# A Flamingo block on one core: the first stage in four pipeline steps, with both layer norms applied by ScalarE

## What is computed

```
x = x + tanh(g_xattn[0]) * L0_xattn(layernorm(x), ctx)      # stage A
x = x + tanh(g_ffn[0])   * L0_ffn(layernorm(x))             # stage B, 8 experts, top 2
x = x + tanh(g_xattn[1]) * L1_xattn(layernorm(x), ctx, ctx) # stage C, 16 heads, mask
x = x + tanh(g_ffn[1])   * L1_ffn(layernorm(x))             # stage D, 8 experts, top 2, and a shared one

layernorm(x) = (x - mean) / sqrt(var + 1e-5)
L0_xattn: q = x1 w_q', k = x2 w_k', v = x2 w_v'; softmax(q k' / sqrt(128)) v
L0_ffn:   logits = x Wg; softmax; the two best experts per token, weights summing to one
```

## Time and profile before

| | |
|---|---|
| median of 3 runs | 770.51 us (768.73 to 771.58) |
| the profiled execution | 768.41 us, of which the span of its instructions is 766.6 us |
| mean granted clock of PE in it | 0.91 of 2.4 GHz |
| stage A in the profiled execution | from 0 to 138.8 us, where stage B's first PE instruction starts |
| busy in the span | PE 656.9 us, DVE 574.7, ACT 427.4, POOL 92.7 |

### The profile page before, as it was taken

How to read it: one execution, slowest core, us unless ns; L and a number is a source line. 1 busy time by engine, 2 the same in 40 slices (tenths; PEclk the granted TensorE clock), 3 DMA queues, 4 the chain that set the end, 5 groups by cost and what they waited for, 6 DMA issues and landing times.

```text
span 766.6 us, 12867 instructions
## 1 busy us (share of the span) xinstructions
PE 656.9 (86%) x4158; PEld 508.3 (66%) x4158; DVE 574.7 (75%) x1211; ACT 427.4 (56%) x657; POOL 92.7 (12%) x121
## 2 busy tenths in 40 slices
PE   5665764799999999995799989989988379999996
PEld 4544553587787778773576766766766258888884
DVE  3777566788898889887586866866866678888885
ACT  3233321577777777773376666665766045555553
POOL 3344221200000000002001011011011100000000
PEclk9677565799999999998599999999999579999998
DMA  5313100000000000002333413413400000000000
GB/s 159 101 53 106 31 8 0 1 1 0 1 0 0 0 0 0 0 1 80 81 99 101 109 37 94 111 37 89 110 1 1 0 1 2 14 14 14 27 15 28
DMA packets 23698, 29.24 MB, mean 38 GB/s; under 512 B 3313, under 2 KB 17522, under 8 KB 23666
## 3 DMA queue, kind: packets, MB, share of 16 engines
q1 hardware_dynamic: 23666, 28.84, 13.3%
HBM read 19.99 MB, written 8.85 MB: 38 GB/s over the span
## 4 chain that ended last, share of the span: by engine, by line
PE 66%; DVE 18%; issue 5%; POOL 5%; ACT 4%; DVEq 1%; DMA 0%; SPq 0%; ACTq 0%; POOLq 0%
PE psum L371 12%; PE psum L373 12%; PE psum L372 12%; PE psum L1156 5%; DVE xn L300 3%; PE psum L1171 3%; DVE stats L281 2%; POOL rstd L293 2%; PE psum L1146 2%; PE psum L360 2%; PE psum L1147 2%; PE psum L1448 2%; PE psum L858 2%; PE psum L349 1%; DVE xl L332 1%
## 5 line engine op out<-in xcount | busy, mean ns | idle before, releaser
L1262 ACT ACTIVATE c_pt<-psum 77x512 f32<-77x512 f32 x128 | 74.9, 586 | 60.5 <-PE psum L1156 60.0
L371 PE MATMUL psum<-xh,w_hi 128*128 (+1 forms) x248 | 102.1, 412 | 2.1 <-DVE d_hr L1536 2.1
L372 PE MATMUL psum<-xl,w_hi 128*128 (+1 forms) x248 | 99.4, 401 | 0.0
L373 PE MATMUL psum<-xh,w_lo 128*128 (+1 forms) x248 | 99.1, 400 | 0.0
L813 DVE TENSOR_TENSOR b_hl<-b_hs,b_hh 128x1024 fp32r<-128x1024 f32 x64 | 78.2, 1222 | 17.9 <-ACT b_hh L807 17.9
L916 ACT ACTIVATE b_hr<-psum,b1s 128x512 f32<-128x512 f32 x128 | 81.1, 686 | 17.1 <-PE psum L373 17.1
L958 DVE TENSOR_TENSOR b_hs<-b_hr,psum 128x1024 f32<-128x1024 f32 x64 | 78.2, 1222 | 12.1 <-ACT b_hr L916 10.9
L807 ACT ACTIVATE b_hh<-b_hs 128x1024 fp32r<-128x1024 f32 x64 | 68.0, 1062 | 34.1 <-PE psum L373 34.1
L1156 PE MATMUL psum<-ident,c_pf 128*77 128x128 f32 x512 | 75.0, 283 | 0.0
L1156 PEld LDWEIGHTS psum<-ident,c_pf 128*77 128x77 f32 x512 | 58.3, 149 | 15.0 <-issue 10.2
L1322 DVE TENSOR_REDUCE c_mx<-psum 128x8 f32<-128x616 f32 x64 | 51.1, 799 | 17.0 <-PE psum L1147 16.0
(11 more groups left out here) (205 smaller groups left out, 1287.5 us busy)
## 6 DMA issues: line engine op xcount, KB each, us to landing
w_hi<-c_q_spread SPq DMA_DIRECT2D x24, 256.0 KB
stage<-in_weights SPq DMA_DIRECT2D x8, 576.0 KB, 4.2
c_q_spread<-w_hi SPq DMA_DIRECT2D x8, 512.0 KB, 3.4
ctxg<-in_ctxT SPq DMA_DIRECT2D x16, 156.0 KB, 4.2
c_k_spread<-w_lo SPq DMA_DIRECT2D x8, 312.0 KB, 2.2
x_all<-in_x SPq DMA_DIRECT2D x8, 256.0 KB, 3.0
out_dram<-x_all SPq DMA_DIRECT2D x8, 256.0 KB, 2.3
c_kb<-c_k_spread SPq DMA_DIRECT2D x48, 39.0 KB
```

The lines of the kernel that those rows point to most:

```text
L371: pe.matmul(o, wh, h, start=start, stop=False)
L372: pe.matmul(o, wh, l, start=False, stop=False)
L373: return pe.matmul(o, wl, h, start=False, stop=stop)
L1262: a_.activation(pt[:, q % NC4, :], bank[2 + q % 2][0:S2, :], ACT.Copy).then_inc(pt_done, 1)
```

## The change

Stage A gets a pipeline of four ages, `step(a, m, t, u)`, in eleven steps: four written out, two rounds of two steps in the loop, three that drain. The group of age `u` does the router's product, copy and transpose, which before were at the end of the step of age `t`. Both layer norms are applied by ACT, as scale times x plus shift with one pointer operand each (four instructions per group and norm), where DVE did it with one subtract-and-multiply instruction per batch. POOL makes the shift, minus mean times inverse root, with two more small instructions per group and norm. POOL now takes `ln0` before `ln1`. DVE's order in a step is statistics of `a`, residual and statistics of `t`, maximum and subtraction of `m`, logits of `u`, sums of `m`, low part of `t`. The router's transposed-back logits go to the PSUM bank of its product. The second part of the routing follows the last low part, and the last part the last logits copy, in a step of its own.

```diff
     step(None, None, Group(None, NG - 1))
 
 
+def pipeline4(eng, step):
+
+    def groups(i, c):
+        return [Group(i, c - k) if c - k >= 0 and (i is not None or c - k < NG) else None for k in range(4)]
+    for c in range(4):
+        step(*groups(None, c))
+    with eng.Fori(0, (NG - 4) // 2) as i:
+        step(*groups(i, 4))
+        step(*groups(i, 5))
+    for c in range(NG, NG + 3):
+        step(*groups(None, c))
+
...
+            def pool_shift(self, q, g, nm):
+                _, m, _, rs, _ = self.bufs
+                p = g.parity
+                q.tensor_scalar(nm[:, p, :], m[:, p, :, 0], -1.0, None, ALU.mult).then_inc(self.centred, 1)
+                q.wait_ge(self.rstd_ready, g.at(1, 1))
+                q.wait_ge(self.centred, g.at(1, 1))
+                q.tensor_tensor(nm[:, p, :], nm[:, p, :], rs[:, p, :], ALU.mult).then_inc(self.moved, 1)
+
+            def act_norm(self, a, g, nm):
+                _, _, _, rs, xo = self.bufs
+                p = g.parity
+                a.wait_ge(self.moved, g.at(1, 1))
+                for t in range(TG):
+                    ins = a.activation(xo[:, p, t, :].rearrange("p (a c) -> p a c", a=1), x_all[:, g.tile(t), :], ACT.Identity,
+                                       bias=nm[:, p, t:t + 1], scale=rs[:, p, t:t + 1])
+                ins.then_inc(self.xn_ready, 1)
...
         def pool_a(q):
-            def step(a, m, t):
+            def step(a, m, t, u):
+                if a:
+                    ln0.pool_rstd(q, a)
+                    ln0.pool_shift(q, a, nm0)
                 if t:
                     ln1.pool_rstd(q, t)
+                    ln1.pool_shift(q, t, nm1)
                 if a:
-                    ln0.pool_rstd(q, a)
                     pool_split(q, a)
-            pipeline(q, step)
+            pipeline4(q, step)
         pool_parts.append(pool_a)
...
 def pe_a(pe):
...
+            def step(a, m, t, u):
                 if m:
+                    scores(m)
+                if u:
+                    if u.i is None and u.c == 0:
+                        pe.wait_ge(s_split, 1)
+                    else:
+                        pe.wait_ge(lg0.lg_copied, u.at(1, 0))
+                    lg0.pe_product(pe, u)
                 if a:
+                    keys_values(a)
+                    ln0.pe_transpose(pe, a)
+                if u:
+                    lg0.pe_transpose(pe, u)
                 if t:
                     ln1.pe_transpose(pe, t)
                 if m:
+                    probs(m)
+                    outs(m)
+            pipeline4(pe, step)
...
         def act_a(a_):
-            def step(a, m, t):
+            def step(a, m, t, u):
                 if a:
                     p = a.parity
                     a_.wait_ge(a_k_ready, a.at(1, 1))
                     a_.activation(A["k0"][:, p, :], bank[1][:, 0:GK], ACT.Copy).then_inc(a_k_done, 1)
                     a_.wait_ge(a_v_ready, a.at(1, 1))
                     a_.activation(A["v0"][:, p, :], bank[2][0:S2, :], ACT.Copy).then_inc(a_v_done, 1)
+                    ln0.act_norm(a_, a, nm0)
+                if u:
+                    lg0.act_copy(a_, u)
+                    if not t:
+                        Route(0, HEAD, rt_tail).act_ratio(a_)
+                if a:
+                    ln0.act_high(a_, a)
+                if t:
+                    ln1.act_norm(a_, t, nm1)
                 if m:
                     p = m.parity
                     a_.wait_ge(a_sub, m.at(1, 1))
                     a_.activation(A["pr"][:, p, :, :], A["sm"][:, p, :, :], ACT.Exp,
                                   bias=zero_col[:, 0:1], scale=float(D) ** -0.5).then_inc(a_exp, 1)
+                if t:
+                    ln1.act_high(a_, t)
+                if m:
                     a_.wait_ge(a_pt_ready, m.at(1, 1))
                     a_.activation(A["pt"][:, p, :], bank[4][0:S2, :], ACT.Copy).then_inc(a_pt_done, 1)
                 if a:
                     act_split(a_, a)
-                if t:
-                    ln1.act_high(a_, t)
-                if a:
-                    ln0.act_high(a_, a)
-                if t:
-                    lg0.act_copy(a_, t)
-                    if not m:
-                        Route(0, HEAD, rt_tail).act_ratio(a_)
-            pipeline(a_, step)
+            pipeline4(a_, step)
...
+            def step(a, m, t, u):
                 if a:
                     wait_apart(v, s_x[a.parity], a.pair(16, 16))
                     ln0.dve_stats(v, a)
-                    ln1.dve_norm(v, t)
-                    if not m:
-                        route.second(v)
-                if a:
-                    if not (a.i is None and a.c < 2):
-                        v.wait_ge(ln0.t_ready, a.at(1, -1))
-                    ln0.dve_norm(v, a)
+                    residual(t)
+                    ln1.dve_stats(v, t)
+                    shift(m)
+                if u:
+                    lg0.dve_copy(v, u)
+                if t and not m:
+                    v.wait_ge(s_split, NG)
+                    v.wait_ge(s_small, 16 * len(small))
+                    v.wait_ge(lg0.lg_copied, NG - 1)
+                    route.first(v)
+                if m:
+                    sums(m)
                 if t:
                     ln1.dve_low(v, t)
                     if not m:
-                        route.weights(v)
-                    lg0.dve_copy(v, t)
-            pipeline(v, step)
+                        route.second(v)
+                if u and not t:
+                    route.weights(v)
+            pipeline4(v, step)
```

More of the change, by code:

```diff
@@ L274, in __init__ @@
                 self.centred = sem(f"{name}_centred")
+                self.moved = sem(f"{name}_shift_ready")
             def dve_stats(self, v, g):
@@ new lines, in scores @@
+            def scores(m):
+                p = m.parity
+                pe.wait_ge(ln0.hi_done, m.at(1, 1))
+                pe.wait_ge(a_k_done, m.at(1, 1))
+                if not (m.i is None and m.c == 0):
+                    pe.wait_ge(a_sub, m.at(1, 0))
+                for b in range(TG):
+                    ins = pe.matmul(bank[3][:, b * SK:(b + 1) * SK], A["xt"][:, p, b * P:(b + 1) * P],
+                                    A["k0"][:, p, b * SK:(b + 1) * SK], start=True, stop=True)
+                ins.then_inc(a_s_ready, 1)
```

139 lines of the change are left out of this document (58 added, 81 removed).

## The result

| | before | after |
|---|---|---|
| median of six runs each, alternating on one chip | 769.67 us (768.37 to 771.58) | 775.72 us (773.81 to 777.66) |
| ratio of after to before | | 1.0078, interval 1.0055 to 1.0100 |
| profiled execution: time, span | 768.4, 766.6 | 777.65, 775.9 |
| first shifted scores (group 0) | 13.78 | 16.29 |
| shifted scores of group 1 | 24.07 | 30.04 |

The change makes the kernel slower by 0.8%, 6.05 us by the medians. The two profiled executions are 9.2 us apart: stage B starts 6.1 us later, and behind stage A there are 631.0 us against 627.8. The loss of the medians then lies in stage A, as far as one execution of each kernel can tell.

The account below looks back on a forecast made before the run. Stage A was taken as bound by waits, no engine full, with DVE on the chain. Start +4.0, six steps -3.2 and end +0.4 gave +1.2 us on 770.5, so 771.7; range 763 to 779.

Parts of the forecast that it names:

- the start: First two steps of stage A, nothing to overlap: 0.5 + 3.5 = +4.0 us.
- the end: End of stage A: dearer last normalisation, shift and last logits wait, less routing blocks off the path: about +0.4 us.
- The circle: Stage A step's chain of waits through PE and ACT: 15.86 us at 1.2 GHz, 14.7 after the clock's give-back.
- give-back of 1.17: In each step, values and first transpose run at the fast clock, together taking 1.17 us off.
- The 3.5 between groups 0 and 1: Start of stage A: group 1's scores follow group 0's after 13.8 us instead of 10.3.
- group 0's shifted scores 0.5 later (dearer normalisation): Start of stage A: the dearer ACT normalisation delays group 0's shifted scores by 0.5 us.
- The routing blocks that left the path: End of stage A: two routing blocks leave the path, 0.7 us for the second and 0.4 assumed for the first.
- A: Rival: fast clock holds over half of PE's run in a step; step 13.7, total 765.7 us; chance 0.16.
- B: Rival: ACT's normalisations cheaper than their rows, 1.2 us for four; step 13.8, total 765.9 us; chance 0.11.
- C: Rival: ACT becomes the bound, four normalisations cost 2.3 us; total 776.9 us; chance 0.15.
- D: Rival: PE never leaves 1.2 GHz before the pauses; step 15.86, total 778.7 us; chance 0.15.
- E: Rival: the floor of POOL's split, 12.4 us, holds the steps; it would only cap a gain; no chance given.

Follow-up runs that it names:

- e2: The changed kernel with only the second normalisation (behind the attention) back on DVE, the first still on ACT: 758.98 us, 0.9867 of the kernel before.
- e1: The changed kernel with both normalisations back on DVE, four ages kept: 742.23 us, 0.9659 of the kernel before.
- e8: The changed kernel with only the first normalisation (ahead of the attention) back on DVE, the second still on ACT: 755.48 us, 0.9836 of the kernel before.
- e11: The kernel before, three ages and normalisations on DVE, with only DVE's and POOL's order as in the change: 764.13 us, 0.9915 of the kernel before.
- e7b: The changed kernel with nine unread identity transposes more per step in PE's pauses: 766.03 us, 0.9973 of the kernel before.
- e4: The changed kernel with the first normalisation on ACT moved ahead of the copies of keys and values: 763.18 us, 0.9928 of the kernel before.
- e5: The changed kernel with the router product behind keys and values and the first normalisation ahead of their copies: 764.32 us, 0.9945 of the kernel before.
- e3: The changed kernel with the router product on PE moved behind keys and values: 767.29 us, 0.9979 of the kernel before.

## What was right and what was wrong in the prediction

I said 771.7 us, no change that can be told, chance 0.43; 763 to 779. It is 775.72, inside the range and 4.0 us above the sum. The ratio's interval, 0.6 to 1.0% slower, lies wholly beyond the 0.5% that I had called no change, so what came is the outcome to which I had given 0.30. The path through the step was forecast rightly. What failed are sizes: the step, the start and the end each came out dearer than in the sum. Against its own execution the sum had +1.2 and stage B's start moved by +6.1.

**The circle was right.** DVE left it, POOL's split is not in it, and the chain has the thirteen links that I had listed. The step came out at 15.09, not 14.7: over six steps -0.8 instead of -3.2, the first error, 2.4 us. In the step of the chain above the outputs take 2.07 (I had 1.69, from the time to the next in a row that followed other work) and the first transpose 0.87 (0.66); the rest sums to 12.1 where I had 12.3. And this is the better kind of step: the two that end at 75.04 and 105.65 take 15.55. In the first of these the values (60.29) still take 1.91 us, so most of the give-back of 1.17 is missing there; in the step shown they take 1.24. So the term that was too small in every step is the outputs, 0.4 us each time, and the give-back of the clock came in full in neither kind of step.

**The start was mis-sized, the second error, 2.0 us.** The 3.5 between groups 0 and 1 were measured as 3.46 (13.75 against 10.29), and this agreement is luck. POOL took up the next root 1.24 us behind group 0's shifted scores (17.53) and not 2, and the maximum of group 1 came 0.8 us after its scores were done (28.78), at 29.55, behind DVE's statistics, a wait that I had at nothing. But "group 0's shifted scores 0.5 later (dearer normalisation)" was 2.5. I priced the normalisation, and not its place: 1.25 for starting at 10.26 instead of 9.01, of which 0.66 is the copy of the values that stands ahead of it on ACT and 0.59 the shift on POOL. The dearer batch itself took 0.52, and the scores' slow matmuls 0.88 (0.13 came back, since the weight copy no longer stands ahead of the transposes' copy). That the copy counts is a rule I had used for the steps and forgot for the start: what stands ahead of the moved work on its new engine counts with it.

**The end: +0.97, not +0.4.** The last logits' wait was 1.03 where I had 0.6. The other terms cancelled: the low part came at the same distance. But they were larger than I had them, and one was missing. e2, with this order and the last normalisation on DVE, has its low part 14.39 behind the last scores (109.43 to 123.82), 2.2 less than before. The routing blocks that left the path make only 0.7 of this (0.5 ahead of the normalisation, 0.2 behind it), where I had 1.1. The greater part, 1.4, lies between the last scores and the residual (8.44 before, 7.01 in e2). Before, DVE could not add the residual until it had copied group 6's router logits:

```profile
123.77 0.19 DVE L366 COPY logits<-psum 128x32 f32<-128x32 f32 x1 [3.54 <-PE psum L360]
```

This wait left with the router's later age, and I had it at nothing. And the ScalarE normalisations cost 2.1 (16.50), where I had 1.0: besides the last group's batch and shift, the batch of the group ahead of it stands before the exponential, so the outputs start 6.10 us behind the last scores (126.68) and not 4.89 (e2).

**The rule of the Trainium skill** ("ScalarE: Activation LUTs", "Rules for kernel authors"), by which this exchange loses, was borne out for the kernel as a whole by e1, e2 and e8: on VectorE it is 33, 17 and 20 us faster. I weighed it only by the 0.5 us by which a batch is dearer. How much it costs depends on the place: in three ages the same exchange took 0.3 to 0.9 from a step, and the whole kernel stayed where it was against the kernel before (0.9988) and lost 0.7% against e11 (0.9915). The stall by GpSimd that spoke for ACT (455 against 340 ns, 1214 against 229, some 1.9 us a step) needed no ACT: in e1 DVE pays nothing either, since the split falls beside statistics and residual. Nor did it need the fourth age: in e11 the same instructions take 336 and 229 ns.

**The rivals.** None came in full. A (the clock holds over half the run, 765.7) would have needed a clock like the one that e7b's idle transposes brought (0.77, 766.0). Its reason, that a denser PE earns the fast level, did not hold in this order: PE's busy share rose from 0.65 to 0.70 and the clock fell from 0.71 to 0.61. B and C are out, the batch costs 1.64. D (never fast, 15.86 a step) is nearest: the truth is a third of the way from the forecast to it in the steps, and the rest of the loss is start and end. E's floor, POOL's split, did not hold the change's steps, but it is what stops e4 and e5, at 13.6 and not 12.4. What I didn't have among them is the wait that e3 and e4 take away, 1.3 to 1.5 us a step: it was in my own sum as "copy 0.50" behind product, keys and values, and I never asked whether the normalisation needed any of these.

**What stays open.** What exactly lets PE's clock rise. In e1 it stood at full level with PE busy for 61% of the steps, in the change at 0.61 with 70%. The same work at the slow level takes longer, so the share of busy time is itself a result. No run here separates cause and effect further than e7b does. Open with it is how e1's gain divides between place and clock.

## What to carry to other kernels

When work moves to another engine, write down what stands ahead of it there and ask of each link of the new circle whether it needs the one before; a batch that is 0.5 us dearer cost 1.8 and 2.9 us a step, by its place and by the clock that went with it. Take a change with several parts apart both ways before judging it: the fourth age lost 0.8 us a step together with the normalisations on ACT and gained 4.3 without. When an edit gives less than its sum, look for the circle that took over: e4 and e5 stopped at POOL's. And where an engine stalls beside another's work, first try to move the order so that they don't meet, before giving the work to a third engine.

## What the runs showed of the hardware

- Useless transposes in PE's pauses raised the granted clock from 0.61 to 0.77 over the steps and made the kernel 1% faster (775.72 to 766.03 us; beside the kernel before 1.0078 and 0.9973).
- The granted clock that is recorded is not to be trusted ahead of its first change. In the change it reads 1.00 until 21.6 us, yet the eight matmuls of the scores at 13.75 take 1.99 us, a duration of the 1.2 GHz level (1.12 at the fast one), and the values at 16.65 take 1.81.
- One ScalarE activation of 128 columns with two pointer operands takes 482 ns, and four overlap to 1.64 us; the prices from bare and one-pointer rows (277 and 0.10 each) gave 477 and 1.64.
- VectorE's `tensor_scalar` with pointers stretches beside GpSimd's subtraction of 1152 columns (four: 3.41 against 1.12 us; the one of four columns, `a_rg`: 1.87 against 0.23), while statistics, aggregation and the residual that ran beside it in e1 kept their 280, 156 and 336 ns.
